# Probabilities of a 16-head attention: split in SBUF and turned by a DMA transpose

## The reference

```python
def _L1_attn_ref(x, Q, K, VO):
    xq = jnp.einsum('btd,hrd->bthr', x, Q)          # 16 heads, rank 64
    xk = jnp.einsum('bud,hrd->buhr', x, K)
    scores = jnp.einsum('bthr,buhr->bthu', xq, xk) / sqrt(dim)
    attn = jax.nn.softmax(scores, axis=3)           # 256 x 256 per batch and head
    return jnp.einsum('bthu,bud,hde->bte', attn, x, VO)
```

## Time and profile before

| | us |
|---|---|
| median of three runs | 632.24 |
| span of the profiled execution | 631.1 |
| TensorE busy (matmuls) | 532.4, 84% |
| VectorE busy | 389.5, 62% |
| ScalarE busy | 301.8, 48% |
| GpSimd busy | 74.7, 12% |
| the 32 heads, first scores to last output | 381.9 to 522.8 |

### The profile page before, as it was taken

The page is one execution under the profiler, slowest core; times in us unless marked ns, Lnnn a source line. Parts: engine busy times, 40 slices in busy tenths (PEclk is TensorE's granted clock), DMA queues, the critical chain, the costliest instruction groups (busy, mean ns, idle before and its releaser), DMA issues.

```text
span 631.1 us, 9189 instructions
## 1 busy us (share of the span) xinstructions
PE 532.4 (84%) x3440; PEld 364.9 (58%) x3440; DVE 389.5 (62%) x833; ACT 301.8 (48%) x654; POOL 74.7 (12%) x61
## 2 busy tenths in 40 slices
PE   4689999699699789878899896988999996448993
PEld 3456675255465346545457674777987893333652
DVE  3675556966364986345665676877777664972235
ACT  2667882417751327771578396676544540011100
POOL 0024130200000200000025322222000000100000
PEclk9999999999999999999999895999999997758997
DMA  5662220000000000001300311122810409320001
GB/s 179 208 198 65 70 92 0 1 0 2 0 1 1 0 2 1 1 0 61 139 2 1 134 34 40 62 68 74 329 54 2 134 1 330 113 91 0 1 0 34
DMA packets 28556, 39.85 MB, mean 63 GB/s; under 512 B 2016, under 2 KB 24544, under 8 KB 28384
## 3 DMA queue, kind: packets, MB, share of 16 engines
q1 hardware_dynamic: 28512, 39.26, 18.7%
HBM read 38.73 MB, written 0.52 MB: 62 GB/s over the span
## 4 chain that ended last, share of the span: by engine, by line
PE 56%; DVE 24%; ACT 12%; issue 4%; DMA 3%; POOL 1%; SPq 0%; DVEq 0%; ACTq 0%; POOLq 0%
PE ps L516 7%; PE ps L545 6%; PE ps L645 4%; PE ps L657 4%; PE ps L530 3%; PE ps L547 3%; PE ps L782 3%; PE ps L804 3%; DMA work<-in_ctx 2%; ACT ctx_tr L1023 2%; PE ps L608 2%; DVE small L1449 2%; DVE ptl L1453 2%; PE ps L620 2%; PE ps L441 1%
## 5 line engine op out<-in xcount | busy, mean ns | idle before, releaser
L516 PE MATMUL ps<-ctx_tr,qtl 128*128 128x512 f16 x384 | 90.6, 379 | 4.8 <-ACT arena L952 3.4
L516 PEld LDWEIGHTS ps<-ctx_tr,qtl 128*128 128x128 f16 x384 | 36.7, 98 | 44.3 <-issue 4.5
L952 ACT ACTIVATE arena<-ps 128x512 f32<-128x512 f32 x64 | 37.9, 595 | 50.7 <-PE ps L516 50.6
L545 PE MATMUL ps<-ctx_nat,pth 128*128 128x512 f16 x172 | 58.6, 379 | 0.3 <-DVE ptl L1353 0.3
L1339 DVE TENSOR_REDUCE mx<-arena 128x1 f32<-128x512 f32 x64 | 43.3, 682 | 21.6 <-ACT arena L952 21.3
L1023 ACT ACTIVATE ctx_tr<-ps,small 128x256 f32<-128x256 f32 x64 | 29.7, 468 | 55.8 <-DVE small L1449 55.8
L937 ACT ACTIVATE arena<-arena,small 128x512 f32<-128x512 f32 x64 | 45.8, 716 | 11.7 <-DVE small L1348 11.7
L657 PE MATMUL ps<-arena,ctx_tr 128*128 128x256 f16 x384 | 47.2, 273 | 0.1
L547 PE MATMUL ps<-ctx_nat,ptl 128*128 128x256 f16 x172 | 46.9, 273 | 0.0
L530 PE MATMUL ps<-const,arena 128*128 128x128 f32 x256 | 39.3, 276 | 8.5 <-ACT arena L937 8.0
L1103 POOL TENSOR_TENSOR rstd<-mv,col 128x2 f32<-128x2 f32 x12 | 9.2, 767 | 305.0 <-DVE mv L1191 305.0
(11 more groups left out here) (259 smaller groups left out, 1120.9 us busy)
## 6 DMA issues: line engine op xcount, KB each, us to landing
work<-in_ctx SPq DMA_DIRECT2D x16, 512.0 KB, 3.7
ctx_nat<-in_w_e SPq DMA_DIRECT2D x8, 1024.0 KB, 6.9
ctx_tr<-in_w_e SPq DMA_DIRECT2D x6, 1024.0 KB, 11.3
work<-in_w_vo SPq DMA_DIRECT2D x8, 512.0 KB, 3.8
ctx_nat<-in_w_l SPq DMA_DIRECT2D x4, 512.0 KB, 6.0
arena<-in_w_e SPq DMA_DIRECT2D x2, 1024.0 KB, 7.0
wts<-in_rows SPq DMA_DIRECT2D x1, 1024.0 KB, 5.6
arena<-in_w_a SPq DMA_DIRECT2D x1, 768.0 KB, 5.1
```

The lines of the kernel that those rows point to most:

```text
L516: mm = pe.matmul(ps[:, n % 2, :], qtl[:, qh, d, u * P:(u + 1) * P], CT[:, d, kh, k0:k0 + CH], start=(i == 0 and d == 0), stop=(i == 2 and ...
L545: pe.matmul(ps[:, acc, :], PH[j % PRING][:, i * P:(i + 1) * P], CN[:, t].rearrange("p h d -> p (h d)"), start=(c == 0 and i == 0), stop=Fa ...
L952: act.activation(S[:, n % SRING, :], ps[:, n % 2, :], ACT.Copy).then_inc(s("score_copied"), 1)
```

## The change

After `norm5` the probabilities are no longer normalised in place. VectorE writes them at once as two float16 halves into `pth` and `ptl`, which now hold one head each, in two slots (`P16`): the high half by a multiplication that rounds, the low half by a fused multiply and subtract, which takes P5, the factor and the high half. The factor 1024 is multiplied into the reciprocal by an instruction of its own. SP then issues one DMA transpose per head, from SBUF to SBUF: [128, 1024] float16 (256 KB) as eight squares of 128x128 into one of three slots (`PT5`). `mix5` waits for that DMA and reads the slot. `turn5` on TensorE, `hi5` on ScalarE and `lo5` on VectorE are gone. A slot of `P16` is written again when the DMA of two heads before has landed, a slot of `PT5` when the mixing of three heads before is done.

SP's loads are interleaved with the transposes.

```diff
+            def turn5(i):
+                sp.wait_ge(s("l_norm"), i + 1)
+                if i >= 3:
+                    sp.wait_ge(s("l_pv"), i - 2)
+                else:
+                    sp.wait_ge(s("l_x_lo"), B)
+                sp.dma_start_transpose(PT5[i % 3].rearrange("p t h u n -> p (t h u) n"),
+                                       P16[i % 2].rearrange("p a n -> p (a n)")).then_inc(s("l_pt%d" % (i % 3)), 16)
...
+            load_vo(2)
+            for i in range(2 * H5):
+                turn5(i)
+                if i % 2 == 0 and i // 2 + 3 < H5 // 2:
+                    load_vo(i // 2 + 3)
+                if i == 13:
...
+                if i in (14, 16, 18, 20):
+                    load_w1(i // 2 - 7)
...
-                def turn5(i):
-                    pe.wait_ge(s("l_norm"), i + 1)
-                    if i >= 2:
-                        pe.wait_ge(s("l_pt_lo"), i - 1)
-                    for u in range(2):
-                        for t in range(2):
-                            mm = pe.transpose(ps[:, 2 + i % 2, (2 * u + t) * P:(2 * u + t + 1) * P],
-                                              P5[:, i % 2, t, u * P:(u + 1) * P], ident)
-                    mm.then_inc(s("l_pt"), 1)
...
-                    pe.wait_ge(s("l_pt_lo"), i + 1)
+                    pe.wait_ge(s("l_pt%d" % (i % 3)), 16 * (i // 3 + 1))
...
-                                               pt[:, i % 2, pu], start=(n == 0), stop=(n == 5))
+                                               PT5[i % 3][:, :, ph, u, :], start=(n == 0), stop=(n == 5))
...
                     if i >= 2:
-                        act.wait_ge(s("l_pt"), i - 1)
+                        act.wait_ge(s("l_norm"), i - 1)
...
                     dve.wait_ge(s("l_exp"), 2 * i + 2)
-                    link(dve.reciprocal(l5[:, i % 2, :], l5[:, i % 2, :]))
+                    if i >= 2:
+                        dve.wait_ge(s("l_pt%d" % ((i - 2) % 3)), 16 * ((i - 2) // 3 + 1))
+                    r = l5[:, i % 2, :]
+                    link(dve.reciprocal(r, r))
+                    link(dve.tensor_scalar(r, r, 1024.0, None, ALU.mult))
+                    cut = P16[i % 2].rearrange("p t (h u) -> p t h u", h=2)
                     for t in range(2):
-                        o = dve.tensor_scalar(P5[:, i % 2, t, :], P5[:, i % 2, t, :], l5[:, i % 2, t:t + 1], 1024.0, ALU.mult, ALU.mult)
+                        o = dve.tensor_scalar(cut[:, t, 0], P5[:, i % 2, t, :], r[:, t:t + 1], None, ALU.mult)
+                    link(o)
+                    for t in range(2):
+                        o = dve.scalar_tensor_tensor(cut[:, t, 1], P5[:, i % 2, t, :], r[:, t:t + 1], cut[:, t, 0], ALU.mult,
+                                                     ALU.subtract)
                     o.then_inc(s("l_norm"), 1)
```

More of the change, by code:

```diff
@@ L205, in build @@
         P5 = ctx_tr[:, 14336:15360].rearrange("p (r t u) -> p r t u", r=2, t=2)
+        P16 = [pth, ptl]
+        PT5 = [qtl.rearrange("p a c n -> p (a c n)")[:, 0:1024], qtl.rearrange("p a c n -> p (a c n)")[:, 1024:2048],
+               work[:, 2048:2560].bitcast(F16)]
+        PT5 = [a.rearrange("p (t h u n) -> p t h u n", t=2, h=2, u=2) for a in PT5]
         oT5 = ctx_tr[:, 15360:16384].bitcast(F16).rearrange("p (r h c n) -> p r h c n", r=2, h=2, c=DC)
@@ L308, in _ @@
                 load_w1(e)
[L309 to L325, removed]
+            load_vo(2)
[4 more added lines that the diff above has]
+                if i == 13:
+                    sp.wait_ge(s("vo_hi"), H5)
+                    sp.wait_ge(s("vo_lo"), H5)
+                    for dst, src in ((w6i, w_in), (w6o, w_out), (wgt, w_gate), (b1c, b_e1)):
+                        sp.dma_start(dst, src).then_inc(s("w6_in"), 16)
+                    for e in range(E6):
+                        sp.dma_start(b2r[64 * (e % 2):64 * (e % 2) + 64, e // 2, :], b_e2[e].partition_broadcast(64))\
+                            .then_inc(s("w6_in"), 16)
+                    sp.dma_start(work[:, 3072:3600], consts6).then_inc(s("w6_in"), 16)
+                if i in (14, 16, 18, 20):
+                    load_w1(i // 2 - 7)
+                if i == H5 + 1:
+                    sp.wait_ge(s("l_pv"), H5)
+                    sp.dma_start(r6, rows6.partition_broadcast(P)).then_inc(s("w6_in"), 16)
+                if i in (27, 29):
+                    sp.wait_ge(s("l_vo"), H5 + H5 // 2)
+                    load_w2(6 if i == 27 else 7)
             sp.wait_ge(s("l_pv"), 2 * H5)
@@ L642, in mix5 @@
                         for u in range(2):
-                            pu = slice(u * SEQ, (u + 1) * SEQ)
-                            for xh, pt in ((0, pth), (1, pth), (0, ptl)):
+                            for xh, ph in ((0, 0), (1, 0), (0, 1)):
                                 mm = pe.matmul(ps[:, 4 + i % 2, d * SEQ:(d + 1) * SEQ], xl5[b][:, xh, u, d * P:(d + 1) * P],
-                                               pt[:, i % 2, pu], start=(n == 0), stop=(n == 5))
+                                               PT5[i % 3][:, :, ph, u, :], start=(n == 0), stop=(n == 5))
                                 n += 1
@@ L668, in low_rank_attention @@
                         scores5(i)
-                    if 0 <= i - 2 < 2 * H5:
-                        turn5(i - 2)
                     if 0 <= i - 3 < 2 * H5:
@@ L1024, in exp5 @@
                                        scale=1.0 / 16, accum_out=l5[:, i % 2, t:t + 1]).then_inc(s("l_exp"), 1)
[L1026 to L1030, removed]
                 def oT(i):
@@ L1040, in low_rank_attention @@
                         exp5(i)
-                    if 0 <= i - 2 < 2 * H5:
-                        hi5(i - 2)
                     if 0 <= i - 3 < 2 * H5:
@@ L1496, in low_rank_attention @@
                         norm5(i - 1)
-                    if 2 <= i <= 2 * H5 + 1:
-                        lo5(i - 2)
                     if i >= 3:
```

4 lines of the change are left out of this document (removed).

## The result

The changed kernel takes 635.84 us (median of 11 runs, 633.06 to 640.17) where the kernel before took 632.89 beside it (11 runs): a ratio of 1.0054 [1.0033, 1.0075]. It is half a per cent slower, and the forecast of 626.1 was wrong. The profiled execution took 634.43 with a span of 632.2, 1.1 over the span of before.

A forecast was written before the change was run, and what follows sets the result against it. TensorE's work bounds all stretches but the first, where ScalarE and VectorE's chain of waits does. Terms -5.0, -1.6, -2.6, -0.9 and +4.0 make -6.1: span 631.1 to 625.0, plus 1.1 gives 626.1 us, range 617 to 657.

The forecast's parts named there:

- the first stretch: Heads 3 to 14: one collision of VectorE with GpSimd's cut gives 4.02 us per head instead of 4.47, -5.0 us.
- The landing: DMA transpose from issue to landing: 4.0 us taken, bounds 2.2 and 12; the forecast is wrong above 5.
- A: DMA transpose slow and setting the pace from a landing of 5.2 us: 639 to 726 us, chance 0.36.
- C: VectorE collides twice with GpSimd per head in heads 3 to 14: 5.2 us per head, 639 us, chance 0.05.
- D: No collision with GpSimd and a quick transpose: 3.28 us per head in all stretches, 615 us, chance 0.07.
- counts only where it stands in the round: ScalarE, busy 11.98 of 22 us: dropping its 512-column copy per head saves time only inside the round of waits.
- SP's queue: 13 issues behind head 13's transpose last 7.7 us; head 14's transpose leaves 4.3 late: +4.0 once, bounds 2.4 and 5.
- Rival E: TensorE's clock could fall to 1.2 GHz after a 4 us stall: adds 3 us, sharing the forecast's range and chance.
- Mostly that is harmless: Transposes sharing SP's order with loads: VO loads of 512 KB do no harm, the next transpose coming over 3.3 us later.
- the third stretch: Heads 20 to 28, with the last layer's entry: 0.43 us of TensorE's work goes per head, -2.6 us, bounds 0 and -3.4.
- The ends: Before the first mixing and after the last scores: 0 at a landing of 4.0 us, one more per microsecond over.
- B: Time about the same, 632 us: at a landing near 5.1 us, SP's run and the ends cancel the savings; chance 0.10.

## Why the prediction was wrong

**The steady pace: right in its value.** Predicted were 4.02 us per head in the first stretch and 3.40 in the second, with 3.28 as the floor. Measured are 3.98, and the floor: 3.24 to 3.28 where no transpose is late. The landing was 3.0 us alone, not 4.0, inside the bounds of 2.2 and 12. The Trainium skill's page "DMA: Bandwidth & Descriptors", "Latency and other measured facts", led to an estimate of 3.5, the nearer one; the 1309 ns per square of "VectorE: DVE Perf Modes", "The three transpose paths", made 10.5 of eight squares in a row, and the trace excludes that. Rivals A, C and D fell with these numbers: no slow transpose, and one collision per head in the first stretch, not two and not none. TensorE's busy time fell by 11.5 us, where 14 was forecast.

**The first stretch: right number, wrong reason.** I added VectorE's list (3.22) and one collision (0.80). But VectorE's list may shrink by 0.2 without effect, as the run without the second wait showed. What sets it is a round of ScalarE and GpSimd, joined by the stretched scaling, in the timeline of after:

```profile
407.56 1.16 POOL L1145 TENSOR_TENSOR arena<-work,arena 128x512 f16<-128x512 f32 x1 [2.82 <-ACT arena L1005]
407.83 0.91 DVE L1447 TENSOR_SCALAR small<-small 128x2 f32<-128x2 f32 x1
...
408.78 0.47 ACT L1029 ACTIVATE ctx_tr<-ps,small 128x256 f32<-128x256 f32 x1 [1.29 <-DVE small L1447]
...
409.69 0.59 ACT L1036 ACTIVATE ctx_tr<-ps 128x512 f16<-128x512 f32 x1
410.17 0.63 ACT L1003 ACTIVATE work<-work 128x512 f32<-128x512 f32 x1
410.83 0.63 ACT L1005 ACTIVATE arena<-work 128x512 f16<-128x512 f32 x1
```

The cut ends at 408.72, and with it the scaling. From there: 0.06 to exp, 0.91 for its two tiles, 0.48 for oT, 0.66 and 0.63 for the two steps on VO, 0.08 to the next cut and 1.16 for it: 3.98. Before, the copy of the turned halves (L1030) stood in the round as well:

```profile
433.54 0.59 ACT L1030 ACTIVATE pth<-ps 128x512 f16<-128x512 f32 x1
434.01 0.60 ACT L1036 ACTIVATE ctx_tr<-ps 128x512 f16<-128x512 f32 x1
```

Its step is 0.47, and 3.98 + 0.47 = 4.45 is within 0.02 of the 4.47 of before. So the 0.80 us between the first stretch of before and the next was not the collision alone, as I had read it; that both are 0.80 is chance. By this sum the gain of the first stretch is that copy, and not TensorE's transposes; no run took the copy alone away. That GpSimd's cut is a part of the round is shown by the run without it. I had written that ScalarE's saving "counts only where it stands in the round"; this is where it did.

**SP's queue: the step that failed.** The term was +4.0 with bounds of 2.4 and 5; heads 17 to 18 show 11.82 - 3.28 = +8.5. The run with the 13 issues put back shows +7.9 at that place and +8.7 in its total. Two parts were missing, the first and the last of these three:
- The lateness was 5.8 us, not 4.3. I let the run begin with transpose 13, but that one's own issue holds SP first (1.23 us; the run begins 1.33 after it, at 439.06), which I had not priced.
- The landing took 3.66 instead of the 3.0 of the steady pace, with the run's loads beside it. The forecast's 4.0 covers this.
- TensorE's next 24 matmuls of 256 columns ran at half clock: 2.74 - 1.31 + 2.56 - 1.31 = 2.7 us. Rival E had this, at 3 us for a stall of this size, but as something apart that could bring the clock down; with the stall forecast, it belonged in the sum.

Counted from the steady 3.28, that makes 4.0 + 1.5 + 0.7 + 2.7 = 8.9, against 8.5; the 0.4 between them is not assigned.

**"Mostly that is harmless" failed too**, for the loads of 1 MB. In the first stretch a head has 4 us, and the expert weights stood there at no cost in three profiles (heads 3 to 14: 43.90 in the changed kernel, 43.89 to 43.95 with four of these loads in it), and at 1.3 and 1.0 us in two others (45.18 and 44.96). From head 14 on it has 3.27, and behind a late transpose, with loads after it, there is no slack: the third stretch (heads 20 to 28) came out at +0.6 where -2.6 was forecast. With those loads gone (the run of 13 issues still in place) it takes 33.74 us, -2.8. So the term for TensorE's work was right, and what was missing is some 3.4 us: the wait behind the loads, and 1.4 of half clock after it (2.74 - 1.31 for the mixings). The run of 13 has a part in this too, since with its small issues early and the same loads in place the stretch takes 34.06. My reading is that the stall brings the bias rows and the next load together. I had asked who uses the loaded data ("only in the last layer"), not who is queued behind the load.

**The ends.** Head 3 came 1.0 us later and the last output 0.4; 0 was forecast for both. The first is a second collision with GpSimd, of the kind of rival C, but once only. VectorE's first pair of low halves starts just ahead of GpSimd's first cut in this loop, takes 1.78 us instead of 0.88, which is 0.9 of the 1.0, and stands in the chain of waits:

```profile
385.98 1.78 DVE L1462 SCALAR_TENSOR_TENSOR pth<-ctx_tr,small,pth 128x256 f16<-128x256 f32 x2
386.05 1.42 POOL L1145 TENSOR_TENSOR arena<-work,arena 128x512 f16<-128x512 f32 x1 [9.47 <-ACT arena L1005]
```

With the measured terms the account closes: -5.3 + (-2.4 + 8.5) + 0.6 - 0.5 + 1.0 + 0.4 = +2.3 for the stage. Of the rivals B was nearest in the difference to the kernel before (0, where +2.9 was measured; A and C had +7), but by another mechanism: it wanted a landing of 5.1. That the total came out near it is chance.

**Open.** The 2.7 us of half clock are read from the steps: no run had the wait without the clock. One megabyte at head 13 costs about 1 us alone and two in a row cost 7: the runs show it, but not from which backlog on. Why the same loads in the first stretch cost nothing in three profiles and 1.0 to 1.3 us in two is open too. And the first stretch with neither the cut nor the loads beside it was not run.

## What to carry over

When a DMA enters the path of the computation, its queue becomes an engine of the loop: list every issue around it with its time (here 0.4 to 0.6 us for a load, 1.23 for a transpose), compare their sum with the loop's period, and do the same with the bytes on the DMA engines. Loads that were free as long as nobody waited behind them must be moved to where the period has slack before the change is judged; here that turned +0.5% into -1.5%. A load must not be moved behind its own first use either: that cost 1.47 us here. And when a stall of several microseconds is forecast, add the slow clock after it.

## What the runs showed of the hardware

- A DMA transpose from SBUF to SBUF of [128, 1024] float16 lands 3.0 us after its issue with nothing beside it, and makes 1056 packets, 1.4 us of all 16 engines. At the rate of the old loads (320 GB/s at a share of 0.85) 256 KB would take 0.7 us, so a transpose costs the engines twice as much time as a load of its size.
- It holds the issuing queue for 1.23 us (2.17 at the most in this stage, beside a load), against 0.42 to 0.60 for each of the 13 loads.
- A load of 1 MB on another engine's queue delays it like one on its own: 6.1 us to landing with only such a load beside it, 4.4 to 7.4 behind loads of its own queue in the changed kernel.
- After waits of 5.2 and 6.2 us TensorE's granted clock was 1.2 GHz for its first 24 matmuls of 256 columns, though it was busy again at once (0.52 over 7 us). After one of 1.5 us it stayed at 2.4 GHz (1.00).
- Beside GpSimd's subtraction of 128x512 (1.16 us), VectorE's scaling of 128x2 mostly takes 0.91 to 1.04 us, and 0.17 elsewhere; a fused pair of 128x256 took 1.78 instead of 0.88.
